# One indirect write of edge keys in flight instead of three, beside an attention layer on one Trainium2 core

## The reference, cut to what matters

```python
q = x @ Wq.T + bq; k = x @ Wk.T + bk; v = x @ Wv.T + bv          # x: (4, 1025, 64)
scores = jnp.einsum('bhnd,bhmd->bhnm', q, k) * SCALE              # 8 heads
attn = jax.nn.softmax(scores, axis=-1)
out = jnp.einsum('bhnm,bhmd->bhnd', attn, v)
h = h + out.transpose(0, 2, 1, 3).reshape(B, N, C) @ Wo.T + bo
...
N_EDGES = 262144
edge_index = jax.random.randint(ks[6], (2, N_EDGES), 0, 16 * 1024, jnp.int32)
h_nodes = (x_flat @ W_gat).reshape(M, HEADS, NUM_EXPERTS)         # M = 4 * 1025 = 4100 nodes
e = jax.nn.leaky_relu(a_src[src] + a_dst[dst], negative_slope=0.2)
denom = jax.ops.segment_sum(jnp.exp(e - e_max[dst]), dst, num_segments=M)
```

## Time and profile before

| | us |
|---|---|
| Median of 3 runs | 5647.86 |
| Lowest and highest of them | 5637.84, 5656.13 |
| Span of the profiled execution, first to last instruction | 5636.4 |
| PE busy in it | 4516.5 (80%) |
| DVE busy | 3521.6 (62%) |
| ACT busy | 2183.2 (39%) |
| POOL busy | 935.3 (17%) |

### The profile page before, as it was taken

How to read it: one execution, slowest core, us unless ns; L and a number is a source line. 1 busy time by engine, 2 the same in 40 slices (tenths; PEclk the granted TensorE clock), 3 DMA queues, 4 the chain that set the end, 5 groups by cost and what they waited for, 6 DMA issues and landing times. The chain is left out here.

```text
span 5636.4 us, 70722 instructions
## 1 busy us (share of the span) xinstructions
PE 4516.5 (80%) x24566; PEld 2743.6 (49%) x24566; DVE 3521.6 (62%) x8760; ACT 2183.2 (39%) x3699; POOL 935.3 (17%) x1106
## 2 busy tenths in 40 slices
PE   7783999999999999999997999995229999972004
PEld 3451444444444444445544555553129988971002
DVE  7556777777777777776544777764115567664325
ACT  1351444444444444444443544453014433331001
POOL 0123111111111111110001000000650000004771
PEclk9555999999999999999987999995569999995556
DMA  2004445665545466745525101101100000000110
GB/s 67 8 1 76 117 126 128 132 138 119 133 123 145 116 133 127 136 122 136 135 88 169 35 24 35 35 1 18 26 2 10 15 15 7 6 4 6 19 14 12
DMA packets 324642, 389.21 MB, mean 69 GB/s; under 512 B 119857, under 2 KB 274749, under 8 KB 323492
## 3 DMA queue, kind: packets, MB, share of 16 engines
q1 hardware_dynamic: 233848, 185.45, 16.2%
q0 software_dynamic: 58368, 172.46, 10.1%
q10 hardware_dynamic: 32076, 26.80, 2.7%
HBM read 313.90 MB, written 70.64 MB: 68 GB/s over the span
## 5 line engine op out<-in xcount | busy, mean ns | idle before, releaser
L1056 PE MATMUL mem_kv<-mem_weights,mem_table 128*128 128x456 f32 x4608 | 1953.2, 545 | 0.0
L1292 DVE SCALAR_TENSOR_TENSOR mem_weights<-mem_above,mem_exps 128x912 f32<-128x912 f32 x1152 | 1273.3, 1105 | 662.3 <-ACT mem_exps L1172 659.3
L1172 ACT ACTIVATE mem_exps<-mem_above 128x912 f32<-128x912 f32 x1152 | 1069.7, 929 | 909.1 <-PE mem_above L1043 908.8
L1056 PEld LDWEIGHTS mem_kv<-mem_weights,mem_table 128*128 128x128 f32 x4608 | 870.1, 189 | 566.0 <-issue 449.9
L2186 DVE TENSOR_REDUCE mha_chunk_max<-mha_max_scores 114x1 f32<-114x342 f32 x864 | 439.1, 513 | 518.8 <-PE mha_max_scores L2054 307.4
L1043 PE MATMUL mem_above<-mem_operands,mem_selector 123*128 123x456 bf16 x2304 | 635.7, 357 | 38.6 <-DVE mem_weights L1292 25.2
L2077 PE MATMUL mha_sums<-mha_probs,mha_value_wide 114*72 114x114 f32 (+1 forms) x5184 | 612.7, 262 | 14.2 <-ACT mha_probs L2168 13.4
L2077 PEld LDWEIGHTS mha_sums<-mha_probs,mha_value_wide 114*72 114x72 f32 (+1 forms) x5184 | 564.9, 144 | 23.7 <-issue 21.3
L2168 ACT ACTIVATE mha_probs<-mha_scores 114x912 f32<-114x912 f32 x324 | 297.5, 930 | 570.5 <-PE mha_scores L2066 372.1
L1043 PEld LDWEIGHTS mem_above<-mem_operands,mem_selector 123*128 123x128 bf16 x2304 | 218.3, 98 | 554.8 <-issue 442.4
L2054 PE MATMUL mha_max_scores<-mha_keys,mha_q 72*114 72x342 bf16 x864 | 277.3, 323 | 225.6 <-issue 172.3
(11 more groups left out here) (588 smaller groups left out, 5294.5 us busy)
## 6 DMA issues: line engine op xcount, KB each, us to landing
mem_table<-in_L_ffn_tables_dram POOLq DMA_DIRECT2D x288, 512.0 KB
mem_operands<-scratch_second_scores SPq DMA_DIRECT2D x216, 256.5 KB
mem_operands<-scratch_first_scores SPq DMA_DIRECT2D x288, 128.2 KB
mem_inv_z<-scratch_inv_z SPq DMA_DIRECT2D x72, 228.0 KB
scratch_second_scores<-mem_sel_parts ACTq DMA_DIRECT2D x81, 171.0 KB
scratch_first_scores<-mem_sel_parts ACTq DMA_DIRECT2D x108, 114.0 KB
scratch_mem_keys<-mem_kvT SPq DMA_DIRECT2D x72, 114.0 KB, 9.4
scratch_mem_values<-mem_value SPq DMA_DIRECT2D x72, 114.0 KB
```

Source lines behind the costliest of these rows:

```text
L1056: last = nc.tensor.matmul(acc[k][:, 0:SPAN], table[:, k, ch, :], W[:, J % 3, c, :], start=(ch == 0), stop=(ch == CHUNKS - 1))
L1172: nc.scalar.activation(E[:, J % 2, :, :], psD[J % 2][:, :, 0:SPAN], ACT.Exp).then_inc(exped, 1)
L1292: nc.vector.scalar_tensor_tensor(W[:, J % 3, :, :], psD[J % 2][:, :, 0:SPAN], 0.0, E[:, J % 2, :, :], ALU.is_ge, ALU.mult).then_inc(weight ...
```

## The change

`SCATTERS` is the number of semaphores among which the columns are dealt out, and so the number of indirect writes that may be under way. It goes from 3 to 1.

```diff
 QBUFS = 3
-SCATTERS = 3
+SCATTERS = 1
```

## The result

| | us | ratio to before, 95% interval |
|---|---|---|
| Before, 4 runs | 5648.3 | |
| After, 4 runs | 5670.16 (5668.5 to 5671.64) | 1.0047, 1.003 to 1.0063 |
| Both once more, on chip d (15 and 6 runs) | 5647.8 and 5669.29 | 1.0038, 1.0025 to 1.005 |

The change makes the kernel some 0.4% slower, where 1.8% faster was forecast (5544). Another chip, f, told at the end of the experiments, puts it at 4.2% slower.

The account below looks back on a forecast made before the run. The prediction took PE, busy nearly throughout except for a 193.6 us stall in unit 0 during the edge writes, to bound the kernel. Stall gone, -193.6, plus a 90 us key wait gave -104: 5544 us, range 5454 to 5850.

Parts of the forecast that it names:

- (1) The stall: Unit 0 of the second attention: PE's late semaphore updates vanish once writes start further apart, -193.6 us.
- the rival with the place: Edge writes: writes to the table starve PE at any pace, so the stall stays, 5846 us; chance 0.20.
- (2) The period: Edge writes on POOL: time P from one start to the next with one in flight, 2.55 us.
- (3) The spare places: Last columns of the edge writes, to neighbouring spare cells: 60 us extra, between 0 and 105.
- second rival: Edge writes: a single write lands slowly, say 4.9 us all along, making PE wait for keys, 5876 us; chance 0.12.
- (4 to 6) The queue behind it: After the writes: POOL through at 4469, keys of b = 2 at 4484, PE waits 90 us in unit 17.
- The mark for no gain: Edge writes: a period P, with everything, of 3.54 us or more means the gain is gone.
- The stall stays: Unit 0: PE starves as long as table columns are written, at any pace, +198 us, 5846; chance 0.20.
- Slow landings: Edge writes: each takes, say, 4.9 us to land, keys come late, +228 us, 5876; chance 0.12.
- Another cause: Start of the second attention: something else holds PE's updates, no change, 5648 us; chance 0.10, with cancelling gain and loss.

Follow-up runs that it names:

- three_spread: Kernel before, three writes in flight, with a column's spare places laid 168 cells apart: 5686.24 us, against 5660.74 for the kernel before on that chip.
- the paced kernels: Kernel before, three in flight, with a POOL memset of 128 x 384, 640 or 128 after each write: 5474.91, 5476.88 and 5627.86 us.
- one_spread: Changed kernel, one write in flight, with a column's spare places laid 168 cells apart instead of side by side: 5500.3 us, ratio 0.9717.
- two_in_flight: Kernel before with SCATTERS = 2, nothing else: 5640.41 us, against 5660.74 for the kernel before on that chip.
- paced_128: Kernel before, three in flight, with a POOL memset of 128 x 128 after each write, starts every 1.36 us: 5627.86 us.
- three_reads: Kernel before with each indirect write replaced by an indirect read of 128 x 4 bytes into a spare tile, edge keys not delivered: 5688.1 us.
- one_spread_early: Changed kernel with spare places 168 cells apart and the keys of b = 2 asked for ahead of column 112: 5483.58 us, ratio 0.9687.
- paced_640: Kernel before, three in flight, with a POOL memset of 128 x 640 after each write, starts every 1.78 us: 5476.88 us, ratio 0.9673.

## Why the prediction was wrong

**(1) The stall: right** on the chip for which it was made. 217.56 - 24.23 = 193.3 us gone from unit 0, against 193.6. The reason given, the pace, held against the rival with the place (three_spread, and the paced kernels). That PE's updates are late, and not DVE's reading of them, has a second witness that the prediction didn't use: ACT, whose exponentials wait for nothing but PE. In PE's and ACT's timelines before, scores that PE ends at 4054.34 are taken 70.2 us later, a longer delay than DVE's 25.

```profile
4053.36 0.98 PE L2066 MATMUL mha_scores<-mha_q,mha_keys 128*114 128x114 bf16 x8
4124.56 0.93 ACT L2168 ACTIVATE mha_probs<-mha_scores 114x912 f32<-114x912 f32 x1 [74.67 <-DMA scratch_mha_k<-mhap_parts]
```

What the rows could not show is that it is a matter of the chip too.

**(2) The period: right.** one_spread has no slow columns: from its second start, 4008.54, to the table's load, 4442.12, it takes 433.6 us for 167 writes, 2.60 each. Forecast 2.55; that is 8 us of the miss. The agreement is partly luck: the usual column takes 2.41 us (median), and 21 of them 3.0 to 4.3, which no term of the sum stood for. The landing itself took 2.1 us at the least and in the median (L2014's line view of one_spread). The 2.0 us of the Trainium skill (DMA: Bandwidth & Descriptors, Anatomy of one DMA — SWDGE (gpsimd) path) agrees with that; the estimate by it, 2.3 for the period, was 0.1 below the median and 0.3 below the mean, the row-based 2.55 nearer to the mean.

**(3) The spare places: the step that failed,** a mis-sized term. The forecast took 60 us for them, between 0 and 105. Measured: from the second start, 3985.89, to 4605.09 are 619.2 us; less the 433.6 of one_spread, 186 us. The bound was wrong and not only the choice within it. It took the 2.63 us between the starts of spare columns in the earlier trace rows as the service of one column, with the fixed part beside it. But with three in flight 2.63 us between starts is 3 x 2.63 = 7.9 us from start to landing, and the three ran side by side: two_in_flight needs 4.3 a column, one in flight 7.9 (7.4 to 8.3 over the last sixteen). The product of number and time stays near 8 (7.9, 8.5, 7.9), as it does for a delay and not for a service. The text had the 7.9 in its second rival, and set it aside for the table columns, where that was right. It should then have set the spare columns at 7.9: 40 of them, at 7.9 - 2.55 each, are 214 us, and the forecast would have been a loss. The prediction named steps (1) and (2) as those where it fails most easily; it failed in (3). And that 5670 still lies within 5454 to 5850 is luck: the upper part of that range stood for a stall that stays, and 0.12 of the chances for slow landings.

**(4 to 6) The queue behind it: right in kind.** The table's load was forecast for 4469 and came at 4605.09; PE's wait was placed in unit 17, for the keys of b = 2, and is there: 219.4 us in place of 90. The excess of 129 is the 126 + 8 us of steps (3) and (2), within 5. The mark for no gain, P = 3.54 with everything, was right: 619.2 / 167 = 3.71, and the stage lost 28.7 us (1073.3 - 1044.6).

**The rivals.** *The stall stays* is out, by the profile after and three_spread. *Slow landings* had the size (5876 at 4.9 us all along) too high, since only spare columns are slow, but it was the mechanism that decided, and 0.12 was too little for it. It came without any load: 0 GB/s in the window from 4400 on. The Trainium skill (DMA: Bandwidth & Descriptors, Latency and other measured facts), which was held against this rival, speaks of a latency that rises with load; it bears on this case neither for nor against. *Another cause* is out where the stall exists: on a chip with it, one in flight removed it, and with three in flight the slower paces left 17.5 and 7.5 us of its 192; the only other thing changed there is the fill, which paced_128 has too.

**What stays open.** Why an indirect DMA every 1.27 us makes PE's semaphore updates 25 us late and more, and why on b and d and not on e and f (nor on c, by one execution), isn't settled. Excluded are the place of the writes, their direction, and the number under way by itself (in the spare columns of the kernel before three are under way, each for 7.9 us, and PE runs at full speed). The stall outlasts the stream in three_reads and three_spread and ends in the kernel before some 45 us after the starts begin to come further apart (4145 to 4191). A backlog of updates would do that; no run shows one directly. Whether plain DMAs at this pace would do it wasn't tried, nor a pace between 1.36 and 1.57. Why neighbouring cells land late isn't shown either. All chips but b were met in one set of runs only, so a state of the machine that holds for an hour isn't excluded.

**The best version.** On chip b, which has the stall, one_spread_early and paced_640 gain 3.1% and 3.3%, with intervals that overlap. On chip f the first is level with the kernel before (1.0013); paced_640 wasn't measured without the stall. Nothing that was measured on c, e or f was clearly faster than the kernel before.

## What to carry to other kernels

With k transfers in flight, the time between two starts can be the landing time divided by k, as it was here (7.9, 4.3 and 2.6 us for k = 1, 2 and 3), and then it is no service time. Before cutting k, multiply that time by k for each part of the stream by itself: the tail of this one landed in 7.9 us and the rest in 2.6 or less. When a stream slows down, look also for what it was pacing: a second, hidden wait (here DVE's for the table) may lie under the first. And if a gap shows no releaser in the profile, run the unedited kernel on a second chip before building a change on it.

## What the runs showed of the hardware

- With one in flight, an indirect write of 128 times 4 bytes to device memory lets the next go 2.4 us after its start (median) when its cells lie 32 or 672 bytes apart, and 7.4 to 8.3 us (last sixteen of the changed kernel) when they are neighbours, with nothing else running (0 GB/s in the window 4400 to 4600).
- Indirect DMAs started every 1.25 to 1.27 us, writes or reads, delay PE's semaphore updates on chips b and d and in the first measurements. DVE takes a search some 25 us late, ACT its scores up to 70 us, while DVE's word reaches PE in 0.04 us. At 1.36 us PE's gaps before a search stay under 16 us; the whole loss is 192 us at 1.27, 168 at 1.36, 17.5 at 1.57 and 7.5 at 1.78 us. On chip e the same program at 1.27 us shows no delay, and the whole kernel takes 180 us less (5470 against 5650), as it does on f and, in one execution, on c.
